# Last attention: projections of q, k and v as three-term products of high and low parts

## The chip, the cores and the metric

The kernel runs on one core of a Trainium2 chip as a single program. The metric is the device time in microseconds (us), the median of several runs. The engines are TensorE (PE in the profile, its weight loads PEld), VectorE (DVE), ScalarE (ACT) and GpSimd (POOL); SyncE (SP) issues the transfers. Each engine takes its own instructions in program order and waits on semaphores for the others.

## What is computed

Four layers, each an attention and a feed-forward part, over 16 batches of 256 tokens with 256 features. Each part is a layer norm, a modulation per batch, the part itself, a gate and an addition to `x`. The change is in the seventh part, the attention of the last layer:

```python
h = _layernorm(x, axis=-1) * (1 + ca) + sa
qkv = h @ w_qkv
q, k, v = split(qkv, 3)                 # to heads of 16
q, k = elu(q) + 1, elu(k) + 1
decay = sigmoid(decay_param)
running_kv   = scan over time: s = decay * s + k * v
running_ksum = scan over time: s = decay * s + k
den = clip(sum over the head of q * running_ksum, 1e-6)
out = (q * running_kv / den) @ w_out
x = x + ga * out
```

## The kernel before

The eight parts are phases that each engine runs one after the other. A phase is a loop over **slots**, one for each of the 16 batches; in slot i an engine does its steps for batch i and, for a software pipeline, steps for the batches before and behind it. The order on an engine is the order in which its `slot` function is written, and nothing else sets it.

The layer norm is a chain over four engines: `ln_stats` (VectorE, `bn_stats` and `bn_aggr`), `ln_rstd` (GpSimd, two small instructions), `ln_apply` (VectorE, writes `xn`), `ln_transpose` (TensorE, four 128x128 transposes of `xn`), `modulate` (ScalarE, two activations that write `hT`). `ahead(step, ..., i, k)` puts the step for batch i + k into slot i, and for batches past the last one it does it for the next phase.

In the last attention (`l3a_tensor`, `l3a_scalar`, `l3a_vector`, `l3a_pool`) a slot i is:

- TensorE: `project` q(i) and k(i), each four f32 matmuls of 128x256 (two rows of the trace each), denominators of i-1 (`l3_qs` by `l3_head`, four matmuls with 8 columns), `project` v(i), the transposes of `xn` for i+1, the output matmuls of i-2, the transposes of `l3_wide` for i-1.
- ScalarE: Relu and Exp of q(i) and of k(i) (`l3_r`, `l3_e`), copy of v(i), `widen` for i-1 (copies the reciprocal denominators out to all features), `modulate` for i+1.
- VectorE: `ln_stats` for i+2, `ln_apply` for i+1, `features` of q(i) and k(i), the scan of k(i) (`l3_sk`), clip and reciprocal of the denominators of i-1, `gated` for i-2 (`y_sb`, waits for the output matmuls of i-2), the scan of kv(i) (`l3_skv`), the product `l3_num` for i-1.
- GpSimd: `ln_rstd` for i+2, `l3_kv`(i) = k times v, `l3_qs`(i), `l3_num`(i) and `add_to_x` for i-2, each an instruction of 128x512.

All buffers named here are single or double (`hT`, `xn`, `y_sb`, `l3_num` have two). The feed-forward of the first layer already has its products in three terms: `matmul3` takes a high and a low part of both operands (f32 values stored as float32r, the low one the rest of the high one) and adds high by high, high by low and low by high, as float32r matmuls. Its high parts are made by VectorE, its low parts by GpSimd.

## Time and profile before

| | us |
|---|---|
| median of 3 runs | 2099.39 |
| runs | 2097.16 to 2099.85 |
| profiled execution | 2101.8 |
| its span, first to last instruction | 2100.0 |
| PE busy | 1850.9 (88%) |
| DVE busy | 1373.0 (65%) |
| POOL busy | 895.8 (43%) |
| ACT busy | 741.1 (35%) |

The last attention reaches from 1753 us (the first projection) to 1912 us of this span. The third feed-forward stands before it, from 1608 us. [...] In a timeline the number in brackets is the idle time in front of an instruction, with what ended it.

### The profile page before, as it was taken

To read this page: it belongs to the slowest core of one execution; us is meant where nothing else is said; L and a number is where in the kernel's file an instruction comes from. 1 tells how busy PE (TensorE), PEld (TensorE's weight loads), DVE (VectorE), ACT (ScalarE), POOL (GpSimd) and SP (SyncE) were. 2 spreads that over 40 slices of the span, in tenths; PEclk is the share of its full clock that TensorE was granted. 3 is DMA by queue.
4 is the path that set the end of the run, shared out by engine and by line. 5 is a ranking of instruction groups with operands and counts; after the bars stand their busy time and mean duration, and the time that the engine had idled before them with its cause. 6 is when DMAs were issued, how large, how long until landed. Compare 5 with 4: busy or idle time off the path is not lost.

```text
span 2100.0 us, 40010 instructions
## 1 busy us (share of the span) xinstructions
PE 1850.9 (88%) x13400; PEld 1270.9 (61%) x13400; DVE 1373.0 (65%) x3587; ACT 741.1 (35%) x1511; POOL 895.8 (43%) x965
## 2 busy tenths in 40 slices
PE   8999999689995999999999968998967888998887
PEld 5555555489993455555555436676756666885443
DVE  4767677465552556565656537888845776886775
ACT  2544444112221465555555531111122223443332
POOL 0345454565653254545454332233333223663233
PEclk7999999799998999999999988999999888999887
DMA  6100000100003745454545300000011000000111
GB/s 230 52 9 5 7 5 9 31 9 8 10 10 68 158 87 106 89 103 90 100 89 103 68 11 9 9 7 7 10 33 43 15 13 17 14 16 13 35 37 40
DMA packets 68177, 93.34 MB, mean 44 GB/s; under 512 B 9852, under 2 KB 62316, under 8 KB 64748
## 3 DMA queue, kind: packets, MB, share of 16 engines
q1 hardware_dynamic: 68076, 92.01, 19.3%
q8 instruction: 61, 1.00, 0.2%
q14 instruction: 40, 0.33, 0.1%
HBM read 61.70 MB, written 29.49 MB: 43 GB/s over the span
## 4 chain that ended last, share of the span: by engine, by line
PE 68%; DVE 19%; issue 6%; POOL 2%; ACT 2%; DMA 2%; SPq 1%; DVEq 1%; POOLq 0%; ACTq 0%
PE PS L1020 16%; PE PS L1965 3%; PE PS L668 3%; PE PS L1841 3%; PE PS L725 3%; PE PS L1175 3%; DVE negmax L2185 2%; PE PS L741 2%; PE PS L507 2%; DVE xn L497 2%; PE PS L722 2%; PE PS L1893 2%; PE PS L1896 2%; PE PS L1945 1%; PE PS L1938 1%
## 5 line engine op out<-in xcount | busy, mean ns | idle before, releaser
L2185 DVE TENSOR_REDUCE negmax<-PS 128x2 f32<-128x512 f32 (+1 forms) x384 | 246.9, 684 | 211.2 <-PE PS L1885 106.0
L538 POOL TENSOR_TENSOR X<-X,y_sb 128x512 f32 (+1 forms) x128 | 165.2, 1291 | 150.1 <-DVE y_sb L533 145.1
L533 DVE TENSOR_TENSOR y_sb<-PS,ga_sb 128x512 f32<-128x512 f32 x96 | 66.2, 690 | 179.0 <-PE PS L769 50.1
L1020 PE MATMUL PS<-we_hi,h_parts 128*128 128x512 f32 x512 | 179.7, 412 | 0.0
L497 DVE TENSOR_SCALAR xn<-X,mv,rs 128x256 f32 (+1 forms) x256 | 155.3, 648 | 22.4 <-POOL rs L490 21.2
L517 ACT ACTIVATE hT<-PS,modT 128x256 f32<-128x256 f32 x256 | 130.0, 559 | 105.6 <-PE PS L507 104.6
L2104 ACT ACTIVATE pw<-PS 128x512 f32<-128x512 f32 x256 | 139.0, 600 | 75.2 <-PE PS L1941 75.2
L488 POOL TENSOR_TENSOR rs<-mv,eps 128x2 f32<-128x2 f32 x128 | 26.6, 208 | 296.3 <-DVE mv L481 296.1
L1020 PE MATMUL PS<-l_h_parts,lut_hi 128*128 128x256 f32 (+1 forms) x768 | 145.5, 291 | 6.7 <-POOL l_h_parts L1143 6.7
L1509 DVE SCALAR_TENSOR_TENSOR l_acc<-PS,rt_g,l_acc 128x256 f32<-128x256 f32 x256 | 106.1, 475 | 30.6 <-PE PS L1020 25.5
L1020 PEld LDWEIGHTS PS<-l_h_parts,lut_hi 128*128 128x128 f32 (+1 forms) x768 | 117.8, 184 | 9.6 <-issue 5.4
L1020 PEld LDWEIGHTS PS<-we_hi,h_parts 128*128 128x128 f32 x512 | 99.1, 194 | 26.5 <-issue 5.9
L1020 PE MATMUL PS<-l_h_parts,lut_lo 128*128 128x256 f32 (+1 forms) x384 | 110.3, 287 | 0.0
L507 PE MATMUL PS<-ident,xn 128*128 128x128 f32 x512 | 82.1, 284 | 31.6 <-DVE xn L497 30.8
L1020 PE MATMUL PS<-we_lo,h_parts 128*128 128x512 f32 x256 | 102.9, 402 | 0.0
L1175 PE MATMUL PS<-hT,l_wqkv 128*128 128x256 f32 x384 | 94.3, 397 | 4.9 <-ACT hT L517 4.0
L1089 ACT ACTIVATE l0f_act<-PS 128x256 f32<-128x256 f32 x96 | 36.8, 383 | 175.1 <-PE PS L1020 175.1
L490 POOL TENSOR_TENSOR rs<-rs,half 128x2 f32<-128x2 f32 x128 | 94.0, 734 | 10.0
L476 DVE BATCH_NORM_STATS2 st<-X 128x6 f32 (+1 forms) x256 | 95.1, 413 | 1.1 <-DMA X<-in_x 0.9
L1152 POOL TENSOR_TENSOR l0f_hid_parts<-l0f_hid,l0f_hid_parts 128x256 fp32r<-128x256 f32 x96 | 72.2, 753 | 50.5 <-DVE l0f_hid_parts L1014 50.0
L507 PEld LDWEIGHTS PS<-ident,xn 128*128 128x128 f32 x512 | 58.4, 143 | 57.0 <-DVE xn L497 38.5
L988 POOL TENSOR_TENSOR l_ms<-l_ms,half 128x32 f32<-128x32 f32 x16 | 87.1, 5442 | 1.3
(270 smaller groups left out, 4383.2 us busy)
## 6 DMA issues: line engine op xcount, KB each, us to landing
ga_sb<-ga_dram SPq DMA_DIRECT2D x128, 128.0 KB, 2.9
qk_dram<-qk_parts SPq DMA_DIRECT2D x64, 192.0 KB, 2.8
KS<-qk_dram SPq DMA_DIRECT2D x32, 384.0 KB, 5.7
QS<-qk_dram SPq DMA_DIRECT2D x32, 384.0 KB, 9.5
qk_dram<-qk_parts SPq DMA_DIRECT2D x64, 128.0 KB, 2.8
wmod<-in_wmod SPq DMA_DIRECT2D x4, 1536.0 KB, 14.0
qk_dram<-qk_parts SPq DMA_DIRECT2D x64, 64.0 KB, 2.5
y_out<-X SPq DMA_DIRECT2D x16, 256.0 KB, 2.2
```

The source lines that it names most:

```text
L476: last_ = dve.bn_stats(st6[b.par][:, t, :], xb(b)[:, t, :])
L490: pool.tensor_tensor(rs[b.par][:, :], rs[b.par][:, :], half[:, 0:TT], ALU.pow).then_inc(s.rstd.sem, 1)
L497: last_ = dve.tensor_scalar(xn[b.par][:, t, :], xb(b)[:, t, :], mv[b.par][:, t, 0:1], rs[b.par][:, t:t + 1], ALU.subtract, ALU.mult)
L507: last_ = pe.transpose(PS[:, 0, kh * T + t * P:kh * T + (t + 1) * P], xn[b.par][:, t, kh * P:(kh + 1) * P], ident[:, :])
L517: last_ = act.activation(hT[b.par][:, kh, :], PS[:, 0, kh * T:(kh + 1) * T], ACT.Identity, bias=modT[:, sub, 0, kh, bass.ds(b.n, 1)], scal ...
L538: pool.tensor_tensor(xb(b), xb(b), y_sb[b.par][:, :, :], ALU.add).then_inc(s.x.sem, 1)
L988: pool.tensor_tensor(ms_sb[:, :], ms_sb[:, :], half[:, 0:TT * HEADS], ALU.pow).then_inc(s.rn.sem, 1)
L1020: last_ = pe.matmul(out, x.bitcast(F32R), y.bitcast(F32R), start=start and n == 0, stop=stop and n == 2)
L1175: last_ = pe.matmul(bank(1 + n)[:, m * T:(m + 1) * T], l3_wqkv[:, kh, n * D + m * P:n * D + (m + 1) * P], hT[b.par][:, kh, :], start=kh == ...
L1509: dve.scalar_tensor_tensor(l1_acc[b.par][:, t, :], bank(1 + (2 * q + t) % 4)[:, e * D:(e + 1) * D], rt_g[b.par][:, t, x_:x_ + 1], l1_acc[b ...
L2104: act.activation(to.rearrange("p a n -> p (a n)"), bank(4 + (2 * n + pr) % 3), ACT.Exp).then_inc(s.prob.sem, 1)
L2185: dve.tensor_reduce(to, src, AX.X, ALU.max, negate=True).then_inc(s.max.sem, 1)
```

## The change

Four things change.

1. **Weights.** GpSimd makes `l3_whi` (high part of `l3_wqkv`, an addition of zero stored as float32r) and `l3_wlo` (the rest), two instructions of 128x1536, once, in slot 2 of the phase before (the third feed-forward), behind `add_to_x` of that slot. TensorE waits for both at the start of its phase.
2. **Activations.** For each batch, ScalarE copies `hT` to the high part `l3_h_parts[:, 0]` right behind `modulate`, and GpSimd subtracts it for the low part `l3_h_parts[:, 1]`, ahead of `l3_kv` in its slot. TensorE's wait at the start of a slot is now for the low part (`h_lo`) and no longer for `hT`.
3. **Products.** Each of the 12 products of a batch is a `matmul3` of three float32r matmuls in place of an f32 matmul.
4. **Order.** On TensorE the transposes of `xn` for i+1 stand right behind q(i) and k(i), no longer behind v(i). On ScalarE `modulate` for i+1 stands before the copy of v(i) and before `widen`, no longer behind them.

```diff
@@ l3a_tensor
             pe.wait_ge(w_in[6], 16 * len(weights[6]))
+            pe.wait_ge(setup["wqkv"], 2)
...
-                        last_ = pe.matmul(bank(1 + n)[:, m * T:(m + 1) * T],
-                                          l3_wqkv[:, kh, n * D + m * P:n * D + (m + 1) * P],
-                                          hT[b.par][:, kh, :], start=kh == 0, stop=kh == 1)
+                        last_ = matmul3(pe, bank(1 + n)[:, m * T:(m + 1) * T],
+                                        [w[:, kh, n * D + m * P:n * D + (m + 1) * P] for w in (l3_whi, l3_wlo)],
+                                        [l3_h_parts[b.par][:, c, kh, :] for c in range(2)], kh == 0, kh == 1)
...
                 if i.ok:
-                    pe.wait_ge(*s.h(i))
+                    pe.wait_ge(*s.h_lo(i))
                     project(i, 0, s.q_ps, s.q)
                     project(i, 1, s.k_ps, s.k)
+                ahead(ln_transpose, pe, pl, i, 1)
                 if (i - 1).ok:
                     denominators(i - 1)
                 if i.ok:
                     project(i, 2, s.hfree, s.v)
-                ahead(ln_transpose, pe, pl, i, 1)
@@ l3a_scalar
+            def high_bits(b):
+                act.wait_ge(*s.h(b))
+                if (b - 2).ok:
+                    act.wait_ge(*s.hfree(b - 2))
+                act.activation(l3_h_parts[b.par][:, 0].bitcast(F32R), hT[b.par][:, :, :], ACT.Copy).then_inc(s.h_hi.sem, 1)
...
                     elu_parts(i, 1, s.k_ps, s.ek)
+                ahead(modulate, act, pl, i, 1)
+                if (i + 1).ok:
+                    high_bits(i + 1)
+                if i.ok:
                     act.wait_ge(*s.hfree(i))
...
                     widen(i - 1)
-                ahead(modulate, act, pl, i, 1)
@@ l3a_pool
                 ahead(ln_rstd, pool, pl, i, 2)
+                if (i + 1).ok:
+                    b = i + 1
+                    pool.wait_ge(*s.h_hi(b))
+                    pool.tensor_tensor(l3_h_parts[b.par][:, 1].bitcast(F32R), hT[b.par][:, :, :], l3_h_parts[b.par][:, 0], ALU.subtract)\
+                        .then_inc(s.h_lo.sem, 1)
@@ plain_pool
                     add_to_x(pool, pl, s, i - 1)
+                if PHASES[first + pl] == "L2_ffn" and pl + 1 < len(sigs) and i.reg is None and i.off == 2:
+                    pool.wait_ge(w_in[6], 16 * len(weights[6]))
+                    pool.tensor_tensor(l3_whi[:, :, :].bitcast(F32R), l3_wqkv[:, :, :],
+                                       zero[:, :].unsqueeze(1).broadcast_to([P, KH, 3 * D]), ALU.add).then_inc(setup["wqkv"], 1)
+                    pool.wait_ge(setup["wqkv"], 1)
+                    pool.tensor_tensor(l3_wlo[:, :, :].bitcast(F32R), l3_wqkv[:, :, :], l3_whi[:, :, :], ALU.subtract)\
+                        .then_inc(setup["wqkv"], 1)
```

TensorE in one slot of the last attention, before: the first row is q and k, then the denominators, v, the transposes of `xn` (L507), the output matmuls and the transposes of `l3_wide`.

```order
L1175 MATMUL PS<-hT,l_wqkv 128x256 x8
L1187 MATMUL PS<-l_head,l_qs 128x8 x4
L1175 MATMUL PS<-hT,l_wqkv 128x256 x4
L507 MATMUL PS<-ident,xn 128x128 x4
L1207 MATMUL PS<-l_wo,l_num 128x256 x4
L1197 MATMUL PS<-ident,l_wide 128x128 x4
```

The same place after, from the last product of k on (L1022 is the line in `matmul3`, L509 the transposes of `xn`, L1190 the denominators; the last rows are the first product of v):

```order
L1022 MATMUL PS<-l_h_parts,l_whi 128x256 x2
L1022 MATMUL PS<-l_h_parts,l_wlo 128x256
L509 MATMUL PS<-ident,xn 128x128 x4
L1190 MATMUL PS<-l_head,l_qs 128x8 x4
L1022 MATMUL PS<-l_h_parts,l_whi 128x256 x2
L1022 MATMUL PS<-l_h_parts,l_wlo 128x256
```

The transposes of `xn` moved from behind v to behind k, in front of the denominators, of v and of the output matmuls.

ScalarE in one slot, before: Relu and Exp twice, `l_v`, `l_wide`, and `modulate` (L517).

```order
L1237 ACTIVATE l_r<-PS 128x512
L1238 ACTIVATE l_e<-PS 128x512
L1237 ACTIVATE l_r<-PS 128x512
L1238 ACTIVATE l_e<-PS 128x512
L1255 ACTIVATE l_v<-PS 128x512
L1244 ACTIVATE l_wide<-l_den 128x512
L517 ACTIVATE hT<-PS,modT 128x256 x2
```

After:

```order
L1240 ACTIVATE l_r<-PS 128x512
L1241 ACTIVATE l_e<-PS 128x512
L1240 ACTIVATE l_r<-PS 128x512
L1241 ACTIVATE l_e<-PS 128x512
L519 ACTIVATE hT<-PS,modT 128x256 x2
L1255 ACTIVATE l_h_parts<-hT 128x512
L1268 ACTIVATE l_v<-PS 128x512
L1247 ACTIVATE l_wide<-l_den 128x512
```

`modulate` (L519) moved ahead of `l_v` and `l_wide`, and the copy to `l_h_parts` came in behind it.

GpSimd in one slot, before:

```order
L488 TENSOR_TENSOR rs<-mv,eps 128x2
L490 TENSOR_TENSOR rs<-rs,half 128x2
L1331 TENSOR_TENSOR l_kv<-l_qk,l_v 128x512
L1336 TENSOR_TENSOR l_qs<-l_qk,l_sk 128x512
L1340 TENSOR_TENSOR l_num<-l_qk,l_skv 128x512
L538 TENSOR_TENSOR X<-X,y_sb 128x512
```

After:

```order
L492 TENSOR_TENSOR rs<-rs,half 128x2
L1340 TENSOR_TENSOR l_h_parts<-hT,l_h_parts 128x512
L1348 TENSOR_TENSOR l_kv<-l_qk,l_v 128x512
L1353 TENSOR_TENSOR l_qs<-l_qk,l_sk 128x512
L1357 TENSOR_TENSOR l_num<-l_qk,l_skv 128x512
L540 TENSOR_TENSOR X<-X,y_sb 128x512
```

The subtraction to `l_h_parts` came in between `ln_rstd` and `l_kv`.

## Rows read from the trace of the kernel before

**Rows 1.** Timeline, one slot: start us, us, engine, line, operation, count, [idle before]
```profile
1828.90 3.72 PE L1175 MATMUL PS<-hT,l_wqkv 128*128 128x256 f32 x16 [0.33 <-ACT hT L517]
...
1831.88 1.54 DVE L497 TENSOR_SCALAR xn<-X,mv,rs 128x256 f32 x2
...
1832.45 0.95 PE L1187 MATMUL PS<-l_head,l_qs 128*128 128x8 f32 x8
...
1833.26 1.97 PE L1175 MATMUL PS<-hT,l_wqkv 128*128 128x256 f32 x8
...
1835.07 0.60 PE L507 MATMUL PS<-ident,xn 128*128 128x128 f32 x4
...
1835.51 1.89 PE L1207 MATMUL PS<-l_wo,l_num 128*128 128x256 f32 x8
...
1837.05 1.00 ACT L517 ACTIVATE hT<-PS,modT 128x256 f32<-128x256 f32 x2
...
1837.24 1.27 POOL L1336 TENSOR_TENSOR l_qs<-l_qk,l_sk 128x512 f32<-128x512 f32 x1
...
1837.63 0.69 DVE L533 TENSOR_TENSOR y_sb<-PS,ga_sb 128x512 f32<-128x512 f32 x1 [1.23 <-PE PS L1207]
...
1838.18 3.72 PE L1175 MATMUL PS<-hT,l_wqkv 128*128 128x256 f32 x16 [0.33 <-ACT hT L517]
1838.24 1.39 DVE L1301 TENSOR_TENSOR_SCAN l_skv<-l_dec,l_kv 128x256 f32<-128x256 f32 x2
...
1840.14 0.74 DVE L476 BATCH_NORM_STATS2 st<-X 128x6 f32 x2
...
1841.02 1.26 POOL L538 TENSOR_TENSOR X<-X,y_sb 128x512 f32 x1
1841.08 1.68 DVE L497 TENSOR_SCALAR xn<-X,mv,rs 128x256 f32 x2
```

**Rows 2.** Windows, last attention's middle: stretch, us, PE busy, PEclk, DMA, GB/s
```profile
1782.00:1894.10 112.10, 108.92 (x580) 1.00 0.06 15
```

**Rows 3.** Timeline, first feed-forward: gate and up products in three terms
```profile
565.90 0.40 PE L1020 MATMUL PS<-l_h_parts,lut_hi 128*128 128x256 f32 x2
...
568.37 0.39 PE L1020 MATMUL PS<-l_h_parts,lut_hi 128*128 128x256 f32 x2
```

**Rows 4.** Groups by line: ScalarE's 128x512 copy, last attention
```profile
L1244 ACT ACTIVATE l_wide<-l_den 128x512 f32<-128x512 f32 x16 | 10.1, 629 | 12.8 <-DVE l_den L1280 12.8
```

**Rows 5.** One line's instructions: GpSimd's low part in first feed-forward, ns min/median/max
```profile
L1143 POOL TENSOR_TENSOR l_h_parts<-hT,l_h_parts x16: 1257/1286/1288, 400.7 to 616.9; 128x512 fp32r<-128x512 f32 x16
```

**Rows 6.** Timeline, last attention's first slots
```profile
1753.30 7.64 PE L1175 MATMUL PS<-hT,l_wqkv 128*128 128x256 f32 x24 [0.78 <-DVE y_sb L533]
1753.32 1.26 POOL L538 TENSOR_TENSOR X<-X,y_sb 128x512 f32<-128x512 f32 x1 [3.76 <-DVE y_sb L533]
...
1763.39 1.27 POOL L1336 TENSOR_TENSOR l_qs<-l_qk,l_sk 128x512 f32<-128x512 f32 x1
1763.46 2.32 DVE L1301 TENSOR_TENSOR_SCAN l_skv<-l_dec,l_kv 128x256 f32<-128x256 f32 x2 [1.10 <-POOL l_kv L1331]
```

**Rows 7.** Windows: TensorE's pauses and the stretches behind them, columns as above
```profile
1558.90:1560.60 1.70, 0.04 (x1) 1.00 0.11 34
1560.60:1564.00 3.40, 3.28 (x20) 1.00 0.08 21
1653.00:1655.50 2.50, 0.02 (x1) 0.97 0.00 0
1655.50:1659.00 3.50, 3.46 (x10) 0.53 0.00 0
...
1737.40:1741.00 3.60, 3.57 (x11) 0.54 0.00 0
```

**Rows 8.** Timeline, GpSimd, third slot of the third feed-forward
```profile
1631.73 1.27 POOL L538 TENSOR_TENSOR X<-X,y_sb 128x512 f32<-128x512 f32 x1
1638.86 0.19 POOL L488 TENSOR_TENSOR rs<-mv,eps 128x2 f32<-128x2 f32 x1 [5.87 <-DVE mv L481]
```

More of the change, by code:

```diff
@@ L242, in build @@
                         "num": 1, "qs": 1, "den_ps": 1, "clip": 1, "rden": 1, "wide": 1, "wide_ps": 1, "o": 1,
-                        "y_ps": 1},
+                        "y_ps": 1, "h_hi": 1, "h_lo": 1},
             "L3_ffn": {"p_ps": 1, "htok_ps": 1, "hsq": 1, "sq": 1, "mx": 1, "ht": 1, "n_ps": 1, "zr": 3, "z": 1, "zT_ps": 1,
@@ L305, in build @@
                                                     "we_hi", "we_lo", "lut_step", "f_ps", "f_step", "f_set", "a_zero", "a_wo", "a_dot", "a_exp", "a_lam",
-                                                    "a_pad", "a_one")}
+                                                    "wqkv", "a_one")}
         wbuf = lambda n, shape, k=2, dt=F32: [sb(f"{n}{i}", shape, dt, work) for i in range(k)]
@@ L447, in build @@
         l3_wide = sb("l3_wide", [P, TT, D], F32, work)
+        l3_whi, l3_wlo = sb("l3_whi", [P, KH, 3 * D], F32, work), sb("l3_wlo", [P, KH, 3 * D], F32, work)
+        l3_h_parts = wbuf("l3_h_parts", [P, 2, KH, T])
         work.close()
```

## Prediction

> **What bounds the kernel now.** I read the timeline of one slot in the middle of the last attention first, then the windows, then the first slots of the phase. The slot is 9.28 us long, from 1828.90 to 1838.18, where q and k start [rows 1]. Over the stretch from 1782.0 to 1894.1, twelve slots, it is 112.1 / 12 = 9.34 us, and TensorE is busy in 108.92 of 112.10 us at a granted clock of 1.00 [rows 2]. So TensorE looks like the bound, and its work in a slot is, by the starts in rows 1: q and k 3.55 (1828.90 to 1832.45), denominators 0.81, v 1.81, transposes of `xn` 0.44, output matmuls and transposes of `l3_wide` about 2.3, together 8.9 us. The rest, 0.33 us, is the wait for `hT`, whose activations stand behind `widen` on ScalarE [rows 1].
>
> The second thing to see is where VectorE stands. It ends `xn` at 1831.88 + 1.54 = 1833.42, 0.97 us **after** k is through TensorE (1832.45), and starts `y_sb` at 1837.63 after 1.23 us of idle, because the output matmuls end then [rows 1]. From that `y_sb` on it runs without a pause: the scan at 1838.24, the statistics at 1840.14, `xn` from 1841.08 to 1842.76 [rows 1]. From the start of `y_sb` to the end of `xn` it takes 5.13 us. Today the transposes of `xn` stand behind v, at 1835.07, 1.65 us after `xn` is ready, so nobody waits for it.
>
> **The products.** Two products of the first feed-forward, 565.90 and 568.37, are seven triples apart: 2.47 / 7 = 0.353 us for a three-term product of 128x256 at full clock [rows 3]. An f32 product is 3.55 / 8 = 0.444 us [rows 1]. The gain is 0.091 us for each of 12 products, 1.1 us of TensorE in a slot. If only TensorE counted, the slot would go to 9.34 - 1.1 = 8.2 us.
>
> **The order: a new loop.** The transposes now stand behind k, in front of denominators, v and output matmuls. All of these wait for `xn`(i+1). `y_sb`(i-2) waits for the output matmuls, and on VectorE the next `xn` stands behind that `y_sb`. That closes a loop within one slot:
> - `xn` done, transposes 0.44, denominators 0.81, v 4 x 0.353 = 1.41, from the start of the output matmuls to `y_sb` 1837.63 - 1835.51 = 2.12 [rows 1, 3]. With 0.1 us for the handoff (estimate: TensorE here stands idle and can't have the transposes queued behind running work) it is 4.9 us.
> - `y_sb`, scan of kv, `l3_num`, statistics, `xn`: 5.13 us as now [rows 1].
>
> The sum is 10.0 us, more than 9.34, though the products are cheaper.
>
> **A dearer scan.** The scan takes 1.39 us where GpSimd's `l3_qs` (1837.24 to 1838.51) covers its first 0.27 us, and 2.32 us in the first slots, where `l3_qs` (1763.39) covers some 1.2 us of it [rows 1, 6]. `xn` is slowed in the same way: 1.68 us beside `X` from 1841.02 on. In the new order GpSimd's chain behind `xn` is: 0.9 us until the transposes are through (0.44 plus their latency, estimate), `hT` 1.00, high part 0.63, low part 1.29, `l3_kv` 1.27, and some 0.3 us of handoffs [rows 1, 4, 5]. That is 5.4 us, and `l3_qs` starts then. The scan starts at 4.9 + 0.6 = 5.5 us. So `l3_qs` covers most of it: overlap 1.1 us in place of 0.27, which I put at +0.6 us (ends: 0, and 2.32 - 1.39 = 0.93). [...] The slot comes to 10.0 + 0.6 = 10.6 us at full clock, 1.25 us more than 9.34. Fifteen slots follow the first: **+19 us** (+10 with no dearer scan, +24 with the full one).
>
> **What else moves.** The high part (0.63 us on ScalarE) and the low part (1.29 us on GpSimd) aren't on that loop [rows 4, 5]: q and k of the next slot could start at about 4.2 us behind `xn`, and TensorE comes to them at 5.5. The wait for the low part stands on GpSimd in front of `l3_kv`, `l3_qs`, `l3_num` and `X`; `l3_kv` is done at 5.4 and the scan asks for it at 5.5, so this second chain is 0.1 us short of deciding. If it decides, it adds a few tenths to a slot, within the range. `widen` behind `modulate` is hidden: `l3_wide` is asked for only after the output matmuls.
>
> **The clock.** TensorE has q and k done long before `xn`: they start 0.55 us behind `y_sb` (1838.18 against 1837.63) and take 8 x 0.353 = 2.8 us, and `xn` is done 5.7 us behind it, so TensorE pauses 2.4 us in each slot. Nothing in this phase shows such a pause today except its start. [...] A pause of 1.7 us at 1558.9 was followed by 1.00 [rows 7]. [...] I take it for three slots of four: 15 x 0.75 x 1.6 = **+18 us** (ends 0 and 24).
>
> **Start of the phase.** q(0) starts at 1753.30 now, 0.75 us behind the last `y_sb` of the phase before, and GpSimd's last `X` of that phase runs from 1753.32 for 1.26 us [rows 6]. The low part of batch 0 stands behind this `X`: 1754.6 + 1.29 = 1755.9. TensorE starts 2.6 us later, and q, k and v of slot 0 take 7.64 us at the low clock in f32 [rows 6], so the products give back little; the serial way by high and low part to q(1) takes the rest. **+3 us** (ends 1 and 4).
>
> **Weights.** Two instructions of 128x1536 on GpSimd are 2 x 3 x 1.27 = 7.6 us by the `X` row [rows 8]. They start when `X` ends, 1633.0, and end at 1640.6; the next `ln_rstd` starts at 1638.86 today [rows 8] and comes some 1.8 us late, of which half a microsecond is slack. VectorE's `xn` of that slot waits. **+1.5 us** (ends 0 and 6, the latter if instructions of VectorE are held for the length of a whole GpSimd instruction, as the scan was in rows 6). The end of the phase gives back about 0.5 us in cheaper products.
>
> **Sum.** 19 + 18 + 3 + 1.5 - 0.5 = +41 us. The profiled execution took 2101.8 us (span 2100.0), 2.4 us above the median of 2099.39; against the median the forecast is 2099.4 + 41 = **2140 us**.
>
> **Rivals.**
> 1. The new loop holds, the clock stays at 1.00: the pauses are too short, or they fall so that no stretch at the low clock follows. 2140 - 18 = 2122 us. For it: behind 1.7 us the clock stayed. Chance 0.22.
> 2. The new loop holds, and low stretches are long. One mechanism would be that a slower TensorE half leaves q and k in the low stretch too. All slots with 1.6 us and some with double: 2150 to 2165 us. Chance 0.13.
> 3. **TensorE stays the bound, and the kernel gets faster.** Place: the wait of the transposes for `xn`(i+1). Price: 15 x (9.34 - 8.2) = 17 us less, plus 4 for start and weights: 2087 us. It decides once `xn` is ready when k ends. It is 0.97 us behind that now, and cheaper products put the end of k 0.7 us earlier, so 1.7 us would have to come from VectorE. For it: VectorE idles 1.23 us before `y_sb` [rows 1]. Against it: that idle time ends with the output matmuls, which now stand behind the transposes themselves. Chance 0.07.
> 4. VectorE and GpSimd fall out of step, so that neither scan nor `xn` is held by GpSimd: the loop is 4.9 + 5.13 less about 1.1 = 8.9 to 9.2 us, and the phase keeps its length within 4 us; with start and weights 2097 to 2104 us. Chance 0.06.
> 5. The change doesn't do what it says: a three-term product costs what the f32 one did. Then v adds 4 x 0.09 = 0.36 us to the loop, 5 us in all, and the sign stays. Folded into the range.
>
> **How the numbers follow.** The forecast has 0.52, for the loop with a low clock in most slots. The low end of the range is rival 1 with a scan only half as dear and a cheap start, 2114; the high end takes the clock in every slot and the dearer ends of scan and weights, 2099.4 + 24 + 24 + 3 + 4 = 2154. Within 0.2% of 2099.4 means 2095 to 2104, about what a measurement of this kernel can tell from no change. Faster 0.08 (rival 3 and the edge of 4), same 0.05, slower 0.87.
>
> **What would show it.** In the profile after: a slot of 10.5 to 12.5 us; TensorE idle over 2 us before the transposes of `xn` in every slot, ended by `xn`; the three-term products at 0.353 us; the scan of kv at 2 us or more beside `l3_qs`; PEclk under 0.9 over the phase; q(0) 2 to 3 us behind `y_sb`. I am wrong about the loop if the transposes start without a wait; about the clock if the windows of the phase show 1.00 with the pauses there; about the scan if it stays at 1.4 us.

## The result, and the profile after

The changed kernel takes 2145.89 us (median of 4 runs, 2142.86 to 2154.38), the kernel before 2098.27 us in the same comparison. The ratio is 1.0234, 95% interval 1.0216 to 1.0253: **slower by 47.6 us**. The profiled execution took 2154.38 us (span 2152.6), 52.6 us over the profiled execution of before.

Where these 52.6 us arise can be read from the starts of VectorE's `y_sb`:

| stretch | before | after | more |
|---|---|---|---|
| up to the last `y_sb` ahead of the third feed-forward | 1607.3 | 1611.6 | 4.3 (before the changed code) |
| from there to the last `y_sb` of the third feed-forward | 145.2 | 151.2 | 5.9 (weights) |
| from there to the last `y_sb` of the last attention | 158.4 | 200.8 | 42.4 |

The first row lies ahead of anything that the change touches. It is spread between runs, and it is most of the 5 us by which the two profiled executions lie further apart (52.6 us) than the medians do (47.6 us).

One slot of the last attention after, timeline, all engines (start us, us, engine, line, operation, output<-input, count, [idle before <- what ended it]); it answers to [rows 1]:

```profile
1827.67 0.65 PE L509 MATMUL PS<-ident,xn 128*128 128x128 f32 x4 [2.50 <-DVE xn L499]
...
1828.36 1.02 ACT L519 ACTIVATE hT<-PS,modT 128x256 f32<-128x256 f32 x2 [2.07 <-PE PS L509]
...
1829.41 0.63 ACT L1255 ACTIVATE l_h_parts<-hT 128x512 fp32r<-128x512 f32 x1
...
1830.12 1.28 POOL L1340 TENSOR_TENSOR l_h_parts<-hT,l_h_parts 128x512 fp32r<-128x512 f32 x1 [1.95 <-ACT l_h_parts L1255]
...
1830.49 1.89 PE L1210 MATMUL PS<-l_wo,l_num 128*128 128x256 f32 x8
...
1831.41 1.27 POOL L1348 TENSOR_TENSOR l_kv<-l_qk,l_v 128x512 f32<-128x512 f32 x1
...
1832.41 0.69 DVE L535 TENSOR_TENSOR y_sb<-PS,ga_sb 128x512 f32<-128x512 f32 x1 [1.82 <-PE PS L1210]
1832.64 1.30 POOL L1353 TENSOR_TENSOR l_qs<-l_qk,l_sk 128x512 f32<-128x512 f32 x1
1833.02 2.05 DVE L1313 TENSOR_TENSOR_SCAN l_skv<-l_dec,l_kv 128x256 f32<-128x256 f32 x2
...
1835.15 1.28 POOL L1357 TENSOR_TENSOR l_num<-l_qk,l_skv 128x512 f32<-128x512 f32 x1 [1.21 <-DVE l_skv L1313]
...
1835.57 0.74 DVE L478 BATCH_NORM_STATS2 st<-X 128x6 f32 x2
...
1836.66 1.46 DVE L499 TENSOR_SCALAR xn<-X,mv,rs 128x256 f32 x2
...
1838.26 0.65 PE L509 MATMUL PS<-ident,xn 128*128 128x128 f32 x4 [2.58 <-DVE xn L499]
```

The slot is 1838.26 - 1827.67 = 10.59 us. TensorE starts the transposes 0.14 us after `xn` ends (1836.66 + 1.46) and has waited 2.58 us for it; before, it was busy nearly without a break. The scan of kv is at 2.05 us where it was 1.39. The second chain, through the low part to `l_kv`, is done at 1832.68, before the scan starts at 1833.02.

Windows from one transposes' start to the next (stretch, its length, then PE, PEld, DVE, ACT, POOL busy with counts, the clock granted to TensorE as a share of its full speed, DMA share, GB/s); they answer to [rows 2]:

```profile
1827.67:1838.26 10.59, 8.01 (x61) 7.56 (x61) 8.59 (x18) 4.94 (x9) 7.35 (x8) 1.00 0.04 13
1838.26:1849.90 11.64, 9.65 (x60) 8.87 (x61) 7.81 (x18) 4.94 (x9) 7.16 (x8) 0.85 0.04 13
...
1888.07:1901.27 13.20, 11.20 (x60) 10.44 (x60) 7.91 (x18) 4.94 (x9) 7.17 (x8) 0.74 0.03 10
```

There are two kinds of slot. Four of the last twelve have a clock of 1.00 and last 10.50 to 10.67 us; the other eight have 0.74 to 0.86 and last 11.6 to 13.2 us. All fifteen together take 176.2 us, where before they took 139.5 (1760.77 to 1900.31).

The weights, GpSimd and VectorE in the third feed-forward's third slot:

```profile
1637.23 2.80 POOL L2454 TENSOR_TENSOR l_whi<-l_wqkv,zero 128x1536 fp32r<-128x1536 f32 x1
1640.11 3.43 POOL L2457 TENSOR_TENSOR l_wlo<-l_wqkv,l_whi 128x1536 fp32r<-128x1536 f32 x1
...
1636.06 4.12 DVE L499 TENSOR_SCALAR xn<-X,mv,rs 128x256 f32<-128x256 f32 x2
...
1640.30 0.17 DVE L1381 TENSOR_REDUCE rt_m<-rt_l 128x2 f32<-128x16 f32 x1
1640.50 3.07 DVE L1382 TENSOR_TENSOR rt_eq<-rt_l,rt_m 128x16 f32<-128x16 f32 x1
```

`xn` ends at 1640.18 and `rt_eq` at 1643.57, each just behind the end of a long GpSimd instruction (1640.03 and 1643.54). `rt_eq` works on 16 columns and takes 0.17 us elsewhere in the same trace. The reduction `rt_m` just before it, which reads one tensor where `rt_eq` reads two, starts beside the same long instruction and keeps its 0.17 us.

### The profile page after: what moved, and what is told of

It reads as the page before. It is cut to its first block, busy times and chain, and to the rows that moved or that the text cites. A ratio compares the mean times of both kernels' runs of the same rounds, so it can differ in the third digit from the quotient of the medians.

```text
span 2152.6 us, 40385 instructions
## 1 busy us (share of the span) xinstructions
PE 1856.2 (86%) x13526; PEld 1293.4 (60%) x13592; DVE 1380.1 (64%) x3587; ACT 751.5 (35%) x1527; POOL 923.8 (43%) x983
## 4 chain that ended last, share of the span: by engine, by line
PE 67%; DVE 19%; issue 6%; POOL 3%; DMA 2%; ACT 2%; SPq 1%; DVEq 1%; POOLq 0%; ACTq 0%
PE PS L1022 18%; PE PS L1982 3%; PE PS L670 3%; PE PS L1858 3%; PE PS L727 2%; DVE xn L499 2%; DVE negmax L2202 2%; PE PS L509 2%; PE PS L743 2%; PE PS L1210 2%; PE PS L724 2%; PE PS L1910 2%; PE PS L1913 2%; PE PS L1955 1%; PE PS L694 1%
## 5 line engine op out<-in xcount | busy, mean ns | idle before, releaser
L1022 PE MATMUL PS<-we_hi,h_parts 128*128 128x512 f32 x512 | 179.8, 412 | 0.0
L519 ACT ACTIVATE hT<-PS,modT 128x256 f32<-128x256 f32 x256 | 130.5, 561 | 139.9 <-PE PS L509 138.9
L499 DVE TENSOR_SCALAR xn<-X,mv,rs 128x256 f32 (+1 forms) x256 | 158.3, 660 | 22.4 <-POOL rs L492 21.3
L1022 PE MATMUL PS<-l_h_parts,lut_hi 128*128 128x256 f32 (+1 forms) x768 | 144.3, 289 | 6.7 <-POOL l_h_parts L1145 6.7
L509 PE MATMUL PS<-ident,xn 128*128 128x128 f32 x512 | 84.1, 288 | 65.0 <-DVE xn L499 64.3
L1022 PEld LDWEIGHTS PS<-l_h_parts,lut_hi 128*128 128x128 f32 (+1 forms) x768 | 116.9, 183 | 9.6 <-issue 5.4
L1022 PEld LDWEIGHTS PS<-we_hi,h_parts 128*128 128x128 f32 x512 | 99.2, 194 | 26.5 <-issue 5.9
L509 PEld LDWEIGHTS PS<-ident,xn 128*128 128x128 f32 x512 | 58.0, 144 | 91.8 <-DVE xn L499 65.8
L1022 PE MATMUL PS<-l_h_parts,lut_lo 128*128 128x256 f32 (+1 forms) x384 | 109.7, 286 | 0.0
L1022 PE MATMUL PS<-we_lo,h_parts 128*128 128x512 f32 x256 | 103.0, 402 | 0.0
L1022 PE MATMUL PS<-l_h_parts,l_whi 128*128 128x256 f32 x384 | 85.8, 324 | 5.5 <-POOL l_h_parts L1340 5.5
```

The lines of the kernel that those rows point to most:

```text
L499: last_ = dve.tensor_scalar(xn[b.par][:, t, :], xb(b)[:, t, :], mv[b.par][:, t, 0:1], rs[b.par][:, t:t + 1], ALU.subtract, ALU.mult)
L509: last_ = pe.transpose(PS[:, 0, kh * T + t * P:kh * T + (t + 1) * P], xn[b.par][:, t, kh * P:(kh + 1) * P], ident[:, :])
L519: last_ = act.activation(hT[b.par][:, kh, :], PS[:, 0, kh * T:(kh + 1) * T], ACT.Identity, bias=modT[:, sub, 0, kh, bass.ds(b.n, 1)], scal ...
L1022: last_ = pe.matmul(out, x.bitcast(F32R), y.bitcast(F32R), start=start and n == 0, stop=stop and n == 2)
```

## Experiments

All ratios are to the kernel before as it ran in the same comparison (its medians there are 2098.2 to 2098.6 us), with 95% intervals. The diffs are shortened to the names of the steps.

| run | us | ratio |
|---|---|---|
| changed kernel | 2145.89 | 1.0234 (1.0216 to 1.0253) |
| e1 order only, float32 | 2127.64 | 1.0129 (1.0103 to 1.0155) |
| e2 transposes back | 2127.09 | 1.0142 (1.0116 to 1.0167) |
| e3 weights in pieces | 2150.29 | 1.0247 (1.0224 to 1.0271) |
| e4 filler | 2129.22 | 1.0138 (1.0113 to 1.0163) |
| e5 norm ahead | 2137.36 | 1.0194 (1.0159 to 1.0229) |
| e6 low behind kv | 2151.43 | 1.0245 (1.0212 to 1.0279) |
| e7 other order | 2126.42 | 1.0141 (1.0112 to 1.0170) |
| e8 float32, norm ahead | 2101.13 | 1.0010 (0.9993 to 1.0028) |
| e9 low on VectorE | 2125.23 | 1.0128 (1.0102 to 1.0154) |
| e10 low copied | 2109.13 | 1.0049 (1.0029 to 1.0068) |
| e11 spare on GpSimd | 2114.93 | 1.0083 (1.0059 to 1.0106) |
| e12 weights only | 2105.80 | 1.0035 (1.0020 to 1.0051) |

### e1: the order alone

The kernel before, with one line moved in TensorE's slot:

```diff
                 project k
+                ahead(ln_transpose, pe, pl, i, 1)
                 denominators(i - 1)
                 project v
-                ahead(ln_transpose, pe, pl, i, 1)
                 output matmuls (i - 2)
```

> The kernel before, float32 products and all, with one edit: TensorE's transposes of the next batch element's normalised rows (xn) stand behind the k product instead of behind v. No high or low parts, no work on GpSimd. Loop theory (the order makes the loop, the parts do not): in one slot xn -> transposes .44 -> denominators .81 -> v 1.81 -> product out to y_sb 2.12, hand-off .1, then VectorE's row from y_sb back to xn 5.1, sum 10.4, and up to 10.7 with the same .27 that the hand sum of the other kernels falls short of. So the slot goes from 9.30 to 10.4-10.7 at the full clock, 15 slots: +17 to +21 us; some slots have a low clock behind a pause that is now some 1.6 us, +0 to +15 us. Time 2115 to 2135, best value 2120, and TensorE's transposes wait 1.4 to 2 us for xn in every slot. Rival (the price lies in the chain high part -> low part -> projections): nothing in that chain is there, so the slot stays 9.3 and the time 2097 to 2101.

Measured: 2127.64 us, +29 us. Timeline and windows of e1, columns as above:

```profile
1811.50 0.66 PE L507 MATMUL PS<-ident,xn 128*128 128x128 f32 x4 [1.67 <-DVE xn L497]
...
1816.54 0.69 DVE L533 TENSOR_TENSOR y_sb<-PS,ga_sb 128x512 f32<-128x512 f32 x1 [2.12 <-PE PS L1207]
1817.15 2.02 DVE L1301 TENSOR_TENSOR_SCAN l_skv<-l_dec,l_kv 128x256 f32<-128x256 f32 x2
...
1811.50:1822.27 10.77, 9.15 (x48) 7.70 (x49) 8.47 (x18) 4.20 (x8) 5.95 (x7) 1.00 0.05 14
1833.13:1845.39 12.26, 10.59 (x49) 8.87 (x49) 8.19 (x18) 4.19 (x8) 5.95 (x7) 0.86 0.04 11
```

The loop is real: with no high or low part anywhere, TensorE waits 1.67 us for `xn` and the slot is 10.8 us. Three of the slots have a low clock, 0.86. The scan of kv takes 2.02 us here too, though there is no low part: with v itself later, the copy of v, `l_kv` and `l_qs` come later. So moving one line costs more than half of what the whole change costs.

### e2: the transposes back, the parts kept

```diff
                 project k
-                ahead(ln_transpose, pe, pl, i, 1)
                 denominators(i - 1)
                 project v
+                ahead(ln_transpose, pe, pl, i, 1)
                 output matmuls (i - 2)
```

> The changed kernel with one edit: TensorE's transposes of xn stand behind v again, as in the kernel before; high part, low part and three-term products stay. Loop theory in its narrow form (only the place of the transposes closes the loop): xn no longer lies before den, v and out in a slot, so the slot falls to what the engines need, 9.3 or less, and the time to 2104 or so. Second-loop theory: with the transposes later, hT, the high part (.6) and the low part (1.29) come later too, and GpSimd, which has the low part first in its row, starts kv, qs and num later; kv -> skv -> xn then closes a loop through GpSimd of about the same length, by hand 10.3 + .27 = 10.55 at the full clock. Then the time stays within 8 us of the changed kernel's 2146, and VectorE's skv or GpSimd's kv waits behind the low part where before they didn't.

Measured: 2127.09 us, between the two forecasts. Rows of e2: windows, then timeline:

```profile
1836.43:1847.22 10.79, 8.40 (x61) 7.51 (x61) 8.99 (x18) 4.89 (x9) 7.34 (x8) 1.00 0.04 13
...
1818.79 1.28 POOL L1348 TENSOR_TENSOR l_kv<-l_qk,l_v 128x512 f32<-128x512 f32 x1
...
1820.11 2.35 DVE L1313 TENSOR_TENSOR_SCAN l_skv<-l_dec,l_kv 128x256 f32<-128x256 f32 x2 [1.53 <-POOL l_kv L1348]
...
1836.43 0.66 PE L509 MATMUL PS<-ident,xn 128*128 128x128 f32 x4 [1.28 <-DVE xn L499]
```

The narrow form of the theory falls: the slot is 10.5 to 10.8 us although the order is the old one. VectorE's scan of kv, which before started right behind `y_sb` [rows 1], now waits 1.53 us for `l_kv`, and `l_kv` stands behind the low part on GpSimd. **So the order alone and the parts alone each make a slot of 10.4 to 10.9 us at 1.00, and together they don't make it longer.** What e2 gains against the changed kernel, 19 us, is the clock: its pauses are 1.0 to 1.3 us, and every slot from 1783.7 on has a clock of 1.00 and 10.4 to 10.8 us. That part I had expected to stay.

### e3: the weights in short instructions

```diff
-  pool.tensor_tensor(l3_whi, l3_wqkv, zero, add)            # 128x1536
+  for n in range(6): pool.tensor_tensor(l3_whi[n], l3_wqkv[n], zero, add)          # 128x256, slot 2
-  pool.tensor_tensor(l3_wlo, l3_wqkv, l3_whi, subtract)     # 128x1536
+  for n in range(6): pool.tensor_tensor(l3_wlo[n], l3_wqkv[n], l3_whi[n], subtract) # 128x256, slot 3
```

> The changed kernel with the high and low parts of the weights made by twelve GpSimd instructions of 128x256 (six in the third FFN's slot 2, six in slot 3) instead of two of 128x1536. Total GpSimd work is the same or more (12 x about .6 to 1.0 us against 6.2). Hold theory: in the changed kernel a VectorE instruction that meets one of the two long ones lasts as long as they do (xn 4.12 us where it had taken 1.69, rt_eq 3.07 where it takes .17), and that, not GpSimd's total, made the third FFN 5.9 us later; with short instructions no VectorE instruction there lasts over 2.2 us, the third FFN takes 3 to 5 us less, and the time is 2141 to 2143. Rival (GpSimd's own time is what delays the FFN): the time stays at 2146 or rises by 1 to 5 us.

Rows of e3, GpSimd and VectorE in the third feed-forward:

```profile
1629.21 3.56 POOL L2456 TENSOR_TENSOR l_whi<-l_wqkv,zero 128x256 fp32r<-128x256 f32 x6
...
1639.70 4.21 POOL L2463 TENSOR_TENSOR l_wlo<-l_wqkv,l_whi 128x256 fp32r<-128x256 f32 x6
...
1628.03 1.99 DVE L499 TENSOR_SCALAR xn<-X,mv,rs 128x256 f32<-128x256 f32 x2
```

GpSimd works longer (7.8 us in place of 6.2), yet no VectorE instruction there lasts over 1.99 us, and the third feed-forward takes 148.6 us (from 1603.55 to 1752.13, ends as in the table above) in place of 151.2. 2.6 us less is a little under the 3 to 5 that I had expected. One whole phase is a coarse measure, though: e7 and e10 have the same twelve pieces and took 150.9 and 151.0 us, e9 147.8, and the kernels with the two long instructions 151.2 to 152.3. The two slots that meet the instructions show it better. They take 24.2 to 24.5 us in every kernel with the long ones, 21.3 to 21.7 us in e3, e7, e9 and e10, and 17.5 us without any. So the hold costs more than GpSimd's own time, and shorter instructions save 3 of the 7 us there; how much of that the whole phase keeps differs from run to run.

The total does not fall: 2150.29 us. In the profiled run the attention behind it took 207.0 us where it took 200.8 in the changed kernel, with only one of its last twelve slots at a clock of 1.00. Whether this is the spread of the low-clock slots or follows from the phase's earlier start isn't settled; the intervals of the two kernels overlap.

### e4: work put into the pause

```diff
                 project k
+                for _ in range(14): pe.matmul(bank(7), l3_whi, l3_h_parts)   # 128x256, read by nobody
                 ahead(ln_transpose, pe, pl, i, 1)
```

> The changed kernel with 14 further float32r products of 128x256 by TensorE in every slot of the last attention, between the k product and the transposes of xn, into a PSUM bank that nobody reads: some 1.65 us of work in the place where TensorE waits 2 to 2.6 us for xn. Nothing of the reference's computation is left out. [...] Rival (the long slots come from the work around VectorE and the low clock is only its companion): slots as long as before, time 2144 to 2150. Third possibility, TensorE too full: 14 products start late and push the transposes, +0 to +10 us.

If the pauses are what brings the low clock, a pause cut down to half a microsecond or one brings it back to 1.00 and the slots to 10.5 to 10.7 us. If the long slots come from elsewhere, they stay.

Measured: 2129.22 us, 16.7 us less than the changed kernel, with 224 matmuls more. Rows of e4: the filler, the transposes behind it, windows:

```profile
1817.18 1.84 PE L1220 MATMUL PS<-l_h_parts,l_whi 128*128 128x256 f32 x14
...
1819.88 0.66 PE L509 MATMUL PS<-ident,xn 128*128 128x128 f32 x4 [0.86 <-DVE xn L499]
...
1830.51:1841.27 10.76, 9.69 (x74) 9.23 (x75) 8.56 (x18) 4.94 (x9) 7.16 (x8) 1.00 0.05 14
1841.27:1852.90 11.63, 11.29 (x75) 10.56 (x75) 7.95 (x18) 4.94 (x9) 7.37 (x8) 0.85 0.04 12
```

The pause is down from 2.5 to 0.9 us, the slots are 10.5 to 10.8 us at 1.00 except two of 11.6. Nothing but TensorE's idle time was changed, so the low clock of the changed kernel came from its pauses, and it is worth 17 us (in the profiled executions, too, the attention takes 183.5 us in place of 200.8). The 14 matmuls took 1.84 us, a little over the 1.65 that I had put.

### e5: the layer norm one slot further ahead

```diff
-                ahead(ln_stats, dve, pl, i, 2)
-                ahead(ln_apply, dve, pl, i, 1)
+                ahead(ln_stats, dve, pl, i, 3)
+                ahead(ln_apply, dve, pl, i, 2)
...
-                ahead(ln_rstd, pool, pl, i, 2)
+                ahead(ln_rstd, pool, pl, i, 3)
```

> The changed kernel with the layer norm of the last attention one slot further ahead: VectorE's statistics and GpSimd's rs three batch elements ahead instead of two, VectorE's xn two ahead instead of one; nothing else moves. Loop theory (the price is that xn is made and used in one slot, with den, v and out behind it): TensorE finds xn ready, its pause in front of the transposes is gone or under .5 us, the clock stays at 1.00, and the slot is set by VectorE's and GpSimd's rows, 9.7 by hand (9.46 + .27). Against 9.30 before: +6 us; the weights +6; the start 0 to 3: 2108 to 2115. Rival (the three added steps hT -> high -> low on two engines are too long for one slot, wherever xn stands): 10.5 at the full clock, 2125 to 2130.

Measured: 2137.36 us, over both forecasts. TensorE's wait for `xn` is gone and the loop through it is open, but the slot stays near 11 us. The timeline of e5 shows what came in its place:

```profile
1841.80 1.78 POOL L1340 TENSOR_TENSOR l_h_parts<-hT,l_h_parts 128x512 fp32r<-128x512 f32 x1
1842.50 3.24 DVE L1302 TENSOR_TENSOR_SCAN l_sk<-l_dec,l_qk 128x256 f32<-128x256 f32 x2
1843.55 1.64 POOL L1348 TENSOR_TENSOR l_kv<-l_qk,l_v 128x512 f32<-128x512 f32 x1
...
1846.92 1.12 PE L1200 MATMUL PS<-ident,l_wide 128*128 128x128 f32 x4 [4.23 <-ACT l_wide L1247]
```

Two scans that take 1.27 us when GpSimd is idle take 3.24 us beside the low part and `l_kv`, and both GpSimd instructions are longer too (1.78 and 1.64 in place of 1.27). TensorE then waits 4.23 us elsewhere, for `l_wide`, and its clock falls (0.86 and 0.91 in windows of two slots). The missing wait had only moved.

### e6: the low part behind kv on GpSimd

```diff
                 ahead(ln_rstd, pool, pl, i, 2)
-                low part (i + 1)
                 kv (i)
+                low part (i + 1)
                 qs (i)
```

> The changed kernel with GpSimd's low part moved one place back in its row, behind kv (kv waits for VectorE's k features and ScalarE's copy of v, which come late in the slot). Theory (the low part must be done before the next slot's q, so its place in front of kv is what the change needs): q starts later by the wait for kv and its 1.28 us, the slot at the full clock goes from 10.55 to 11.4, +13 us, and TensorE's idle time in front of q lets the clock fall about as often as now, or oftener, 0 to +12: 2156 to 2172. Rival 1 (GpSimd is idle a third of the slot, so the place does not matter): 2143 to 2149. Rival 2 (kv -> skv -> xn is the longer branch, and kv first shortens it): slot 10 and fewer low-clock slots, 2125 to 2140.

Measured: 2151.43 us (1.0212 to 1.0279), 5.5 us over the changed kernel, with overlapping intervals. Windows of e6 from one `y_sb` to the next:

```profile
1857.70:1868.90 11.20, 8.32 (x63) 7.63 (x61) 8.97 (x17) 4.94 (x9) 7.11 (x7) 1.00 0.04 12
1868.90:1882.00 13.10, 9.76 (x62) 9.01 (x60) 9.51 (x18) 4.93 (x9) 7.67 (x9) 0.87 0.03 10
```

Cut at `y_sb`, a slot at 1.00 is 10.9 to 11.2 us, some 0.5 over the changed kernel's, half of what I expected; cut at the transposes it is 11.5 to 11.8 us, about what I expected (11.4). The first place in GpSimd's row looks like the better one, by little; the experiment doesn't separate the theory from rival 1 by the time.

### e7: another order for the same arithmetic

```diff
 TensorE:  transposes(i+1), k, q, den(i-1), v, output(i-2), row of 1/den(i-1)
 ScalarE:  modulate(i+1), k parts, q parts, copy of v, high part(i+1), widen(i-1)
 VectorE:  stats(i+3), k features, 1/den(i-1), xn(i+2), scan k, q features, y_sb(i-2), scan kv, l3_num(i-1)
 GpSimd:   rs(i+3), low part(i+1), kv, qs, num, X(i-2); weights in twelve instructions
```

> The changed kernel's arithmetic in another order: layer norm one slot further ahead (as in the run e5), TensorE's row transposes, k, q, den, v, out, row of 1/den; ScalarE modulates first and makes the high part behind its q and k work; VectorE takes k's features first and 1/den earlier; GpSimd's q sums wait for q themselves; weights in twelve short GpSimd instructions. TensorE's own work in a slot is now 7.9 us where with float32 products it is 9.0. Theory (the three-term product is cheaper, and only the order hides it): slot 8.6 (8.34 + .27 by hand), 15 x -.7 = -10 against before, weights +3, start 0 to 3: 2090 to 2098, below the kernel before. [...]

Measured: 2126.42 us; the slot is 10.7 us (mean of twelve) where 8.6 was expected. That is the clearest miss, and the most useful row. Windows, then timeline of e7:

```profile
1830.00:1840.60 10.60, 8.64 (x61) 7.44 (x61) 10.51 (x18) 4.89 (x10) 8.55 (x8) 1.00 0.08 13
...
1851.22 1.28 POOL L540 TENSOR_TENSOR X<-X,y_sb 128x512 f32 x1
1851.35 1.69 DVE L1281 SCALAR_TENSOR_TENSOR l_qk<-l_e,l_r 128x512 f32<-128x512 f32 x1
...
1853.45 0.64 DVE L499 TENSOR_SCALAR xn<-X,mv,rs 128x256 f32 x2
1853.86 1.89 POOL L1340 TENSOR_TENSOR l_h_parts<-hT,l_h_parts 128x512 fp32r<-128x512 f32 x1
1854.00 2.29 DVE L1303 TENSOR_TENSOR_SCAN l_sk<-l_dec,l_qk 128x256 f32<-128x256 f32 x2
1855.71 1.68 POOL L1348 TENSOR_TENSOR l_kv<-l_qk,l_v 128x512 f32<-128x512 f32 x1
```

VectorE is busy 10.51 of 10.60 us, and not because it has more to do. The features, 0.66 us by themselves, start 0.13 us behind `X` and last 1.69 us, until `X` is over and 0.6 us more. The low part starts while `xn` and a scan run and lasts 1.89 us; the second scan then waits for it. In these rows the instructions of the two engines go **by turns**. Their lengths when undisturbed add up to: VectorE two features 1.3, four scans 2.55, `xn` 0.65, GpSimd five long instructions, one every 1.25 us, 6.25: together 10.75 us. Without the low part it is 9.5, and the slot of before was 9.3. Two of VectorE's instructions don't take part, in the changed kernel's slot above: `y_sb`, which reads a PSUM bank, starts at 1832.41, while `l_kv` still runs, and takes its 0.69 us; the statistics, which read one tensor, start at 1835.57 beside `l_num` and take 0.74 us, as before [rows 1]. So they are not in the sum.

### e8: the same room for float32

```diff
 before, with stats(i+3), xn(i+2), rs(i+3); transposes behind k as in e1; modulate(i+1) ahead of the copy of v
```

> The kernel before (float32 products) with the layer norm one slot further ahead and the transposes behind k, as a fair companion of e5 and e7. Theory (before, TensorE bounds the slot: 3 x 1.81 for q, k and v + .83 + .47 + 1.76 + .5 = 9.0, and 9.30 is what stood): with the same order as the changed kernel but xn ready, the loop is gone, the slot is 9.1 to 9.4 and the time 2094 to 2101; e1's 29 us vanish whole. Rival (the place of the transposes costs by itself, by displacing v and out): 2110 or more.

Measured: 2101.13 us, no different from before (0.9993 to 1.0028). Twelve slots take 110.7 us, 9.2 each (from `y_sb` to `y_sb`, 1783.95 to 1894.61; before, 111.1 us). A window of about two slots:

```profile
1829.90:1848.60 18.70, 17.96 (x96) 15.37 (x96) 17.13 (x35) 8.72 (x17) 12.05 (x14) 1.00 0.06 14
```

The 29 us of e1 are gone once `xn` is made a slot earlier. (e8 also moves `modulate` ahead, which e1 doesn't; that edit has no run of its own.) The same step left the three-term kernel at 2137. What stands between e8 and e5 are the three-term products and the work that makes their parts.

### e9, e10, e11: the turns, tested from three sides

e9: e7, with the low part on VectorE.

```diff
-                    pool.tensor_tensor(low part, hT, high part, subtract)     # GpSimd
+                    dve.tensor_tensor(low part, hT, high part, subtract)      # VectorE, behind the k features
```

> The order of run e7 with one edit: the low part is a VectorE instruction (behind the k features) and no longer one of GpSimd. Turn theory, formed from e7 (VectorE is busy 10.5 of 10.6 us there, its scans 2.3 us instead of 1.27 and its features 1.7 instead of .66 when they meet a GpSimd instruction of 1.27): VectorE's instructions on two SBUF sources and GpSimd's long ones run one at a time, so a slot cannot be shorter than their sum: features 1.3, scans 2.55, xn .65 and GpSimd's five of 1.25 = 10.75 for e7, four of 1.25 = 9.5 for the kernel before. With the low part on VectorE (.66 instead of 1.25) the sum is 10.1 and by hand the slot 9.7 to 10.1: 15 x -.7 = -10 against e7's 2126: 2112 to 2120. Rival (VectorE is simply overloaded): .66 more for it, slot 11.2, 2135.

e10: e7, with the low part a second copy by ScalarE (the subtraction is left out).

```diff
-                    pool.tensor_tensor(low part, hT, high part, subtract)
+                    act.activation(low part, hT, Copy)
```

> The order of run e7, but the low part is a second copy of hT by ScalarE instead of the subtraction on GpSimd: the subtraction is left out, the three-term products stay as long as they were. Nothing of the three-term scheme then needs VectorE or GpSimd. Turn theory: the sum is 9.5 again as in the kernel before, by hand the slot is 9.3 to 9.5 although TensorE has only 7.9 us of work: -1.2 x 15 = -18 against e7, 2104 to 2110, above the kernel before by the weights. Rival (only TensorE and the waits count, VectorE and GpSimd run freely side by side): 8.7, 2094 to 2098.

e11: e8, with one more GpSimd instruction that nobody waits for.

```diff
                 ahead(ln_rstd, pool, pl, i, 3)
+                pool.tensor_tensor(l3_spare, l3_wqkv[:, 0, :512], l3_wqkv[:, 1, :512], subtract)
                 kv (i)
```

> Run e8 (float32 products, slot 9.2, 2101) with one more GpSimd instruction in every slot of the last attention, where the changed kernel has the low part: a subtraction of 128x512 float32 from two SBUF sources into a buffer that nobody reads. It waits for nothing and nobody waits for it; GpSimd is idle a third of the slot. Turn theory: VectorE's two-source instructions wait for it by turns, the sum goes from 9.5 to 10.75 and the slot from 9.2 to 10.2-10.6: +15 to +20 us, 2116 to 2122, with VectorE busy nearly the whole slot. Rival (GpSimd has 3 us to spare): 2099 to 2103.

Windows of four slots of e9, e10 and e11, in this order:

```profile
1829.90:1870.90 41.00, 32.73 (x240) 29.56 (x240) 40.61 (x72) 19.54 (x37) 26.92 (x24) 1.00 0.05 13
```

```profile
1820.00:1858.80 38.80, 33.38 (x242) 29.96 (x241) 38.42 (x69) 21.82 (x40) 26.72 (x25) 1.00 0.05 14
```

```profile
1822.00:1863.20 41.20, 36.13 (x194) 30.92 (x194) 38.34 (x70) 17.23 (x32) 30.16 (x28) 1.00 0.05 13
```

And the timeline of e11, GpSimd and VectorE:

```profile
1846.33 1.79 POOL L1329 TENSOR_TENSOR l_spare<-l_wqkv 128x512 f32<-128x512 f32 x1
...
1847.03 3.25 DVE L1292 TENSOR_TENSOR_SCAN l_sk<-l_dec,l_qk 128x256 f32<-128x256 f32 x2
```

| kernel | sum of undisturbed lengths | slot measured (mean of 12) | us, forecast | us, measured |
|---|---|---|---|---|
| e7, low part on GpSimd | 10.75 | 10.7 | 2090 to 2098, without the sum | 2126 |
| e11, float32 + spare | 10.75 | 10.3 | 2116 to 2122 | 2115 |
| e9, low part on VectorE | 10.1 | 10.25 | 2112 to 2120 | 2125 |
| e10, low part on ScalarE | 9.5 | 9.7 | 2104 to 2110 | 2109 |
| e8, float32 | 9.5 | 9.2 | 2094 to 2101, without the sum | 2101 |
| before, float32 | 9.5 | 9.25 | | 2098 |

The sum gives each slot within half a microsecond, and tells the slots over 10 us from those under 10. It is a yardstick and not a floor: four of the six slots are shorter than their sum, by up to 0.45 us. The theory that the engines run freely side by side (8.7 for e10, no longer than e8 for e11) is refuted by both. In e11 the spare instruction has no data in common with anything, GpSimd had room for it, and still the slot grew by 1.1 us, with the scans at 3.25 us.

e9 missed in its time much more than in its slot (10.25 us against 9.7 to 10.1). The slots shortened by 0.4 us, some 6 us in all, but from the last `y_sb` of the feed-forward to the first of the attention e9 takes 38.6 us and e7 33.9. There VectorE waits up to 3.7 us for the high part, and the clock is lower in two slots (0.91 and 0.80, where e7 has 1.00); which of the two does it has no run of its own. e10 shows that what is left without the low part is still above the kernel before, though TensorE is busy only 8.3 us of a slot of 9.7. VectorE is busy or held in 38.42 of 38.80 us there.

The traces show it without a sum, too. In one or two slots at a clock of 1.00 near 1840 us of the kernel before, the changed kernel, e2, e7, e8, e9, e10 and e11, VectorE and GpSimd are both idle for less than 0.1 us of a slot (time in which one is held by the other counts as busy). In e1 they are both idle for 1.1 us at a stretch (1814.42 to 1815.54), while TensorE does v and the output matmuls: there the loop through TensorE alone sets the slot.

### e12: the weights alone

```diff
 the kernel before
+  in the third feed-forward, slot 2: l3_whi and l3_wlo made by GpSimd (two instructions of 128x1536), read by nobody
```

> The kernel before plus only the two GpSimd instructions of 128x1536 that make the high and low parts of the weights in the third FFN; nobody reads them. Hold theory, from the changed kernel's trace (xn 4.12 us, rt_eq 3.07 us beside them, third FFN 151.2 us from its first to its last y_sb against 145.2): the last attention starts 5 to 6 us later and keeps its slots of 9.3, time 2103 to 2106. Rival (the prediction's own figure, GpSimd's time counted only where it sticks out): +1.5, 2100.

Measured: 2105.80 us, +7.6 us (+4 to +11 by the interval). Rows of e12:

```profile
1627.15 3.42 POOL L2441 TENSOR_TENSOR l_wlo<-l_wqkv,l_whi 128x1536 fp32r<-128x1536 f32 x1
...
1627.54 3.06 DVE L1366 TENSOR_TENSOR rt_eq<-rt_l,rt_m 128x16 f32<-128x16 f32 x1
```

The feed-forward takes 151.2 us, as in the changed kernel, and the attention behind it has the slots of the kernel before (9.0, 9.4, 9.0, 9.7 and so on). This term stands by itself: 5.9 us in the trace.

## Why the prediction was right, point by point

**The slot at full clock: right in size, only half right in cause.** The working gave 10.0 + 0.6 = 10.6 us; the slots at 1.00 are 10.50 to 10.67. Each piece is in the trace: from the end of `xn` to `y_sb` it is 4.8 us (4.9 forecast), from there to the end of the next `xn` 5.7 us (5.7 forecast), TensorE waits 2.5 us for `xn` (2.4 forecast), a three-term product takes 0.358 us (1833.01 to 1835.16, six products; 0.353 forecast), the scan of kv 2.05 us beside `l_qs` (2.0 forecast). Three steps had no row behind them. Two came out near: the handoff to the transposes (0.1 us forecast, 0.14 measured) and the time until the transposes are through (0.9 us forecast, 0.69 from 1827.67 to 1828.36). The handoffs from `hT` over high and low part to `l_kv` were put at 0.3 us and are 0.12 (1829.38 to 1829.41, 1830.04 to 1830.12, 1831.40 to 1831.41). The slot of before was read a little too long: the twelve slots from 1782.03 end at 1893.09, 9.26 us each and not 9.34, so the step puts the cost of the loop 1 us too low over fifteen slots. e1 shows that the loop by itself gives 10.8 us, and e8 that it vanishes with `xn` made earlier.

What the prediction did not see is how little the loop matters. It had the other chain, through the low part to `l_kv` and the scan, "0.1 us short of deciding", and in the changed kernel `l_kv` is in fact done 0.3 us before the scan starts. But e2 shows a slot of the same length with the first loop opened, the scan now waiting 1.53 us for `l_kv`, and e7 shows that behind both stands a third limit, the turns of VectorE and GpSimd. All three come to 10.5 to 10.8 us here; that the one that was worked out gives the right length is in part luck. Whoever had read the forecast as "put the transposes back and it is fast" would have been wrong by 23 us (2127 in place of 2104).

**The dearer scan.** The step took one scan into account, beside `l3_qs`. The size was right (2.05 us), though e1 has the same scan at 2.02 us without a low part, so the high and low parts in front of `l_kv`, from which the step was worked out, aren't needed for it. One scan was too narrow a view: beside a GpSimd instruction of this size the features take 1.69 us in place of 0.66 (e7), `xn` 1.68 in place of 0.64 ([rows 1], e7), the pair of scans of k 3.24 and 3.25 in place of 1.27 (e5, e11), and GpSimd pays in turn, with 1.64 to 1.89 us in place of 1.27 (e5, e7). In the changed kernel's order features and first scan run while GpSimd waits for the high part (1.95 us idle), so that only the scan of kv and `xn` pay, and the sum came out right.

**The clock: right in its total.** +18 us forecast, as 15 x 0.75 x 1.6. Measured in the trace: 176.2 - 15 x 10.55 = 18 us. Measured by e4: 16.7 us. No run shows the 1.6 us, nor the three slots of four, for a slot of this phase. The two stretches of 0.53 and 0.54 in [rows 7] lose about as much (3.50 x 0.47 and 3.60 x 0.46, 1.6 to 1.7 us), in the phase before. What the runs showed in their place made up for each other: of the last twelve slots eight were low and not nine, and they lost 2.0 us each and not 1.6. Four of them, at 0.84 to 0.86, lost 1.1 to 1.4 us, and four, at 0.74 to 0.75, lost 2.6 to 2.7, which is the doubled loss of rival 2. Pauses of up to 1.7 us were followed by 1.00 in most slots (e1: all but three; e2 from 1783.7 on and e4, up to 1.3 us: all but two of e4), pauses of 1.7 to 2.7 us in the changed kernel by a low clock in eight slots of the last twelve. The length of the single pause does not decide it: the four slots at 1.00 stand behind pauses of 2.4 to 2.7 us, and the eight at 0.74 to 0.86 behind 1.7 to 2.6. The shorter ones are presumably so because TensorE, busy 9.6 to 11.2 us in a low slot in place of 8.0, comes later to the transposes. So rival 1 (2122) would have been the result with pauses of about 1 us, and e2 and e4 are that rival, at 2127 and 2129.

**Start and end of the phase.** Forecast +3 and -0.5. q(0) starts 3.4 us behind the last `y_sb` (1766.15 against 1762.75), 2.65 us later than before, as the step had it; the low part stands behind `X` on GpSimd:

```profile
1763.52 1.26 POOL L540 TENSOR_TENSOR X<-X,y_sb 128x512 f32<-128x512 f32 x1 [3.32 <-DVE y_sb L535]
1764.74 1.27 POOL L1340 TENSOR_TENSOR l_h_parts<-hT,l_h_parts 128x512 fp32r<-128x512 f32 x1
...
1766.15 0.77 PE L1022 MATMUL PS<-l_h_parts,l_whi 128*128 128x256 f32 x2 [3.44 <-POOL l_h_parts L1340]
```

What is left of the 42.4 us beside the fifteen slots (36.7) is 5.7 us, over the 2.5 of the two terms. Nearly all of it is the end. From the last `y_sb` of the feed-forward to the transposes of slot 0 it is 8.7 us in place of 8.2, though q(0) starts 2.65 us later, since the transposes no longer wait for v; from the last transposes to the last `y_sb` it is 15.95 us in place of 10.6. So the end did not give back 0.5 us, it took 5.4: behind the last transposes there is now den, v and output work that used to lie in front of them.

**The weights: the mis-sized term.** Forecast +1.5 us with an upper end of 6, "if instructions of VectorE are held for the length of a whole GpSimd instruction". That condition holds, and the term is 5.9 us in the trace and in e12's. GpSimd's own time was over-estimated (6.2 us, not 7.6), what hung on it was missed: an instruction of 0.17 us lasted 3.07. (The high end of the range, 2154, was added up with 3 and 4 us beside the slots and the clock; the terms' own upper ends, 4 for the start and 6 for the weights, would have given 2157.)

**The sum.** The terms as measured in the trace are 42.4 + 5.9 = 48.3 us (by the medians 47.6) against a forecast of 41. The 7.3 us that were missing are 4.4 for the weights and 3.2 for start and end; the slots were 0.3 under. Rival 3 (TensorE stays the bound, 2087) fell by e7 as well: in an order made for it the slot is 10.7 us, and in e10, with the low part off both engines, still 9.7. No version tried with three-term products is faster than the kernel before. By the sum none with this split of work between VectorE and GpSimd should be, which is argued from the kernels of the table and not shown for all.

What stays open: whether in e2 the chain through `l_kv` or the turns set the slot (both give about 10.7), what sets the 9.25 us of the kernel before, where TensorE is busy 8.9 to 9.2 us of a slot and VectorE and GpSimd between them all of it, and why e3's attention took 6 us longer than the changed kernel's.
